# Message passing over a sorted graph on one core: table products in 36 of 40 steps, and one masking per five gathered tiles

## The reference

```python
h = relu(layernorm(x))
att = sigmoid(h[src] @ W_att[:d] + h[dst] @ W_att[d:] + b_att)
messages = (h[src] @ W_msg + b_msg) * att
aggregated = segment_sum(messages, dst, num_segments=num_nodes)
gi = aggregated @ W_ih.T + b_ih
gh = h @ W_hh.T + b_hh
r = sigmoid(i_r + h_r); z = sigmoid(i_z + h_z); n = tanh(i_n + r * h_n)
h_new = (1 - z) * n + z * h
out = x + gamma * (h_new - mean(h_new)) * rsqrt(var(h_new) + eps) + beta
```

## Time and profile before

| | |
|---|---|
| runs | 2367.26 us median of 3 (2366.56 to 2371.25) |
| the profiled execution | 2366.6 us |
| its span, first to last instruction | 2364.5 us |
| mean granted TensorE clock | 0.905 of full speed |
| busy share | PE 89%, DVE 83%, ACT 82%, POOL 75% |
| first gather of the 1600 starts, last one starts | 151.3 us, 2302.1 us |

### The profile page before, as it was taken

The page is one execution under the profiler, slowest core; times in us unless marked ns, Lnnn a source line. Parts: engine busy times, 40 slices in busy tenths (PEclk is TensorE's granted clock), DMA queues, the critical chain, the costliest instruction groups (busy, mean ns, idle before and its releaser), DMA issues.

```text
span 2364.5 us, 52153 instructions
## 1 busy us (share of the span) xinstructions
PE 2099.6 (89%) x17348; PEld 2019.7 (85%) x17348; DVE 1971.8 (83%) x4410; ACT 1931.7 (82%) x6704; POOL 1761.8 (75%) x1713
## 2 busy tenths in 40 slices
PE   3527999999999999999999999999999999999987
PEld 3426989989989989989989989989989989989977
DVE  6948888888888888888888888888888888888874
ACT  2378989989989989989989988989989989989934
POOL 5777777777777777777777777777777777777770
PEclk9856989989989989989989989989989989989988
DMA  9942222222222222222222222222222222222245
GB/s 172 276 99 72 58 63 61 59 62 61 61 63 64 59 62 61 59 62 61 59 62 62 63 62 61 59 62 61 59 62 62 61 64 62 58 63 60 58 124 202
DMA packets 175040, 178.53 MB, mean 76 GB/s; under 512 B 85953, under 2 KB 137203, under 8 KB 174643
## 3 DMA queue, kind: packets, MB, share of 16 engines
q0 software_dynamic: 54272, 112.04, 21.4%
q1 hardware_dynamic: 114121, 60.96, 10.0%
q10 hardware_dynamic: 6378, 2.18, 0.7%
HBM read 148.71 MB, written 26.33 MB: 74 GB/s over the span
## 4 chain that ended last, share of the span: by engine, by line
PE 59%; ACT 23%; DVE 8%; issue 4%; POOL 3%; DMA 2%; ACTq 1%; DVEq 0%; POOLq 0%
PE ps L1429 36%; ACT big L889 18%; PE ps L1414 9%; PE ps L1424 8%; ACT gate_ring L885 4%; POOL big L751 2%; PE ps L1435 2%; PE ps L1436 2%; DVE big L1181 2%; DMA row_ring<-node_table,set_idx 2%; DVE gate_ring L1165 1%; POOL row_ring L760 1%; PE ps L1438 1%; PE ps L1437 1%; DVE n_blk L1192 1%
## 5 line engine op out<-in xcount | busy, mean ns | idle before, releaser
L760 POOL DMA_INDIRECT row_ring<-node_table,set_idx x1600 | 1658.2, 1036 | 493.8 <-issue 380.3
L889 ACT ACTIVATE big<-set_score,big 128x128 f32<-128x128 f32 x4704 | 1506.6, 394 | 109.0 <-PE ps L1429 108.8
L1429 PE MATMUL ps<-big 128*128 128x128 f32 x9408 | 1366.8, 285 | 0.0
L1429 PEld LDWEIGHTS ps<-big 128*128 128x128 f32 x9408 | 1196.1, 197 | 0.0
L1181 DVE TENSOR_TENSOR big<-ps,big 128x784 f32<-128x784 f32 x768 | 743.2, 968 | 5.4 <-ACT big L889 2.8
L1414 PE MATMUL ps<-gate_ring,row_ring 128*128 128x64 f32 x3200 | 611.0, 275 | 119.7 <-DVE gate_ring L1165 118.9
L1165 DVE SCALAR_TENSOR_TENSOR gate_ring<-lane,set_rel,gate_ring 128x64 f32<-128x64 f32 x1600 | 453.2, 283 | 295.6 <-ACT gate_ring L885 287.9
L885 ACT ACTIVATE gate_ring<-set_win,row_ring 128x64 f32<-128x64 f32 x1600 | 537.0, 342 | 192.4 <-DMA row_ring<-node_table,set_idx 171.6
L1414 PEld LDWEIGHTS ps<-gate_ring,row_ring 128*128 128x128 f32 x3200 | 521.3, 205 | 178.7 <-DVE gate_ring L1165 171.5
L1424 PE MATMUL ps<-key_hot,lo_hot 128*128 128x196 bf16 x3072 | 411.0, 258 | 45.2 <-DVE big L1181 26.0
L1151 DVE TENSOR_TENSOR key_hot<-lane_key,set_key 128x1568 bf16<-128x1568 bf16 x384 | 372.2, 969 | 0.0
(11 more groups left out here) (124 smaller groups left out, 936.4 us busy)
## 6 DMA issues: line engine op xcount, KB each, us to landing
row_ring<-node_table,set_idx POOLq DMA_INDIRECT x1600
big<-in_x_dram SPq DMA_DIRECT2D x48, 256.0 KB, 6.1
h_blk<-hT_spill SPq DMA_DIRECT2D x97, 64.0 KB
node_table<-big SPq DMA_DIRECT2D x24, 258.0 KB
hT_spill<-big SPq DMA_DIRECT2D x24, 256.0 KB, 5.7
out_dram<-big SPq DMA_DIRECT2D x24, 256.0 KB
set_win<-dst_scores SPq DMA_DIRECT2D x160, 32.0 KB
set_score<-dst_scores SPq DMA_DIRECT2D x48, 64.0 KB, 2.9
```

The lines of the kernel that those rows point to most:

```text
L760: nc.gpsimd.indirect_dma_start(row_ring[:, t % ROWS_RING, :], None, table, bass.IndirectOffsetOnAxis(ap=set_idx[:, t // SET % 2, t % SET:t ...
L889: return nc.scalar.activation(a_buf[b % 2][:, h, :], set_score[:, b % 2, :], ACT.Sigmoid, bias=m_all[:, h, D:ROW])
L1429: return nc.tensor.matmul(ps[:, AM_BANK, 0:P], m_all[:, h, 0:D], a_buf[b % 2][:, h, :], start=h == 0, stop=h == HI - 1)
```

## The change

- **Products and gates in 36 steps.** `PARTS` goes from 32 to 36, `DENSE_AT` from 8 to 7. The table products are made in steps 3 to 38, two or three in each. ScalarE's gates for block u + 1 begin at step 7 of unit u and end at step 2 of unit u + 1.
- **`keep_block`** moves from step 38 of the same unit to step 1 of the next, ahead of the last `keep_pairs`.
- **One masking per five tiles.** `mask` (128x64 in f32, one per tile) is replaced by `make_masks` (is-equal over five tiles, 128x320, bf16 in and out, into `mask_ring`) and `gate_masks` (128x320, bf16 mask times f32 gates in place). `make_masks` of tiles 5m to 5m + 4 stands at the step of tile 5m + 2, `gate_masks` at that of tile 5m + 5, and TensorE's five `scatter` of them at that of tile 5m + 6. Before, tile t was masked and multiplied at its own step.
- **Rings.** `row_ring` has 13 buffers for 10, `gate_ring` 10 for 8. A group's sum is added one tile later (`GROUP_LAG`).
- **Destinations in bf16**, each twice, in the same bytes: four copies of 128x400 in the set-up (L800) become eight.

```diff
-PARTS = 32
+PARTS = 36
 PARTS_AT = 3
-DENSE_AT = 8
-GROUP_LAG = 3
+DENSE_AT = 7
+GROUP_LAG = 4
+MASKS = 5
...
-ROWS_RING = 10
-GATES_RING = 8
+ROWS_RING = 13
+GATES_RING = 10
...
+def masks_at(u, s, lag):
+
+    t = SPARSE - LAST_TILES + s if u == BLOCKS else tile_at(u, s)
+    return (t - lag) // MASKS - 1 if t is not None and t % MASKS == lag and MASKS <= t < SPARSE + MASKS else None
...
+def dense_at(u, s):
+
+    return (u + 1, s - DENSE_AT) if s >= DENSE_AT else (u, s + STEPS_U - DENSE_AT)
...
 def slices_of(part, total):
-    more = total % PARTS
-    first = part * (total // PARTS) + min(part, more)
-    return range(first, first + total // PARTS + (part < more))
+    return range(part * total // PARTS, (part + 1) * total // PARTS)
...
-                    if u + 1 < BLOCKS and s >= DENSE_AT:
-                        i = s - DENSE_AT
+                    b, i = dense_at(u, s)
+                    if 0 < b < BLOCKS and i < PARTS:
...
-            def mask(t):
-                dve.wait_ge(gates_ready, t + 1)
-                hot = gate_ring[:, t % GATES_RING, :]
-                nc.vector.scalar_tensor_tensor(out=hot, in0=lane[:, :], scalar=set_rel[:, t // SET % 2, t % SET:t % SET + 1],
-                                               in1=hot, op0=ALU.is_equal, op1=ALU.mult).then_inc(masks_ready, 1)
+            def make_masks(m):
+                first = 2 * (m * MASKS % SET)
+                rel = set_rel[:, m * MASKS // SET % 2, first:first + 2 * MASKS]
+                wait_reuse(dve, masks_ready, m - 1)
+                nc.vector.tensor_tensor(
+                    mask_ring[:, m % 2, :, :, :],
+                    lane_key[:, 0:WIN].rearrange("p (h w) -> p h w", w=2).unsqueeze(1).broadcast_to((P, MASKS, WIN // 2, 2)),
+                    rel.rearrange("p (j w) -> p j w", w=2).unsqueeze(2).broadcast_to((P, MASKS, WIN // 2, 2)),
+                    ALU.is_equal).then_inc(masks_made, 1)
+
+            def gate_masks(m):
+                dve.wait_ge(masks_made, m + 1)
+                dve.wait_ge(gates_ready, (m + 1) * MASKS)
+                at = m * MASKS % GATES_RING
+                hot = gate_ring[:, at:at + MASKS, :]
+                nc.vector.tensor_tensor(hot, mask_ring[:, m % 2, :, :, :].rearrange("p j h w -> p j (h w)"), hot, ALU.mult
+                                        ).then_inc(masks_ready, 1)
...
-                        mask(t)
+                        if t % MASKS == 2:
+                            make_masks(t // MASKS)
                         if t % GROUP == GROUP_LAG and t > GROUP:
                             add_group(t // GROUP - 1, bases[t // GROUP - 1])
+                    m = masks_at(u, s, 0)
+                    if m is not None:
+                        gate_masks(m)
...
+                    if s == 1 and u > 1:
+                        keep_block(u - 2)
...
-                    if s == STEPS_U - 2 and u:
-                        keep_block(u - 1)
...
-                pe.wait_ge(masks_ready, t + 1)
+                pe.wait_ge(masks_ready, t // MASKS + 1)
...
-                    t = tile_at(u, s)
-                    if t is not None:
-                        scatter(t)
+                    m = masks_at(u, s, 1)
+                    if m is not None:
+                        for t in range(m * MASKS, (m + 1) * MASKS):
+                            scatter(t)
```

More of the change, by code:

```diff
@@ L152, in gnn_program @@
     assert TILES % 2 == 1 and SPARSE < TILES and FINE <= P and GROWS <= P and HI <= P and 5 * GROWS <= 512 and KEYS <= 256
-    assert SPARSE % SET == 0 and GROUPS % 2 == 0 and DENSE_AT + PARTS == STEPS_U and SETS > 2 and TILES % 16 == 5
+    assert SPARSE % SET == 0 and SET % MASKS == 0 and GROUP % MASKS == 0 and GATES_RING % MASKS == 0 and LAST_TILES % MASKS == 0 and GROUPS % 2 == 0 and DENSE_AT + PARTS < STEPS_U + 4 and PARTS_AT + PARTS < STEPS_U and SETS > 2 and TILES % 16 == 5
     assert B_FIRST < HI and first_tile(1) >= GATES_EARLY and ZEROED <= D0 and -(-STEPS // 5) <= WIN and all(
@@ L161, in gnn_program @@
     idx_dram = nc.dram_tensor("sparse_src", (P, SPARSE), U32, kind="Internal").ap()
-    rel_dram = nc.dram_tensor("sparse_dst", (P, SPARSE), F32, kind="Internal").ap()
+    rel_dram = nc.dram_tensor("sparse_dst", (P, 2 * SPARSE), BF16, kind="Internal").ap()
     lo_dram = nc.dram_tensor("dense_lo", (P, QTILES), BF16, kind="Internal").ap()
@@ L288, in gnn_program @@
         set_idx = sb("set_idx", [P, 2, SET], U32)
-        set_rel = sb("set_rel", [P, 2, SET])
+        set_rel = sb("set_rel", [P, 2, 2 * SET], BF16)
         set_lo = sb("set_lo", [P, 2, PAIRS_B], BF16)
@@ L295, in gnn_program @@
         gate_ring = sb("gate_ring", [P, GATES_RING, WIN])
+        mask_ring = sb("mask_ring", [P, 2, MASKS, WIN // 2, 2], BF16)
         lo_hot = sb("lo_hot", [P, 2, BATCH // 2, P, 2], BF16)
@@ L381, in gnn_program @@
         gates_ready = sem("gates_ready")
+        masks_made = sem("masks_made")
         masks_ready = sem("masks_ready")
@@ L580, in _ @@
                     sp.dma_start(idx_dram, idx_cols.bitcast(U32)).then_inc(sparse_stored, 16)
-                    sp.dma_start(rel_dram, rel_cols).then_inc(sparse_stored, 16)
+                    sp.dma_start(rel_dram, rel_cols.bitcast(BF16)).then_inc(sparse_stored, 16)
                 if c == 21:
@@ L798, in keep_edges @@
                     c, j = e % 4 // 2, 5 * (e % 2)
-                    cols = (idx_cols.bitcast(U32) if e < 4 else rel_cols)[:, c * GROWS * GROUP:(c + 1) * GROWS * GROUP]
-                    nc.scalar.copy(cols.rearrange("e (p j) -> e j p", j=GROUP)[:, j:j + 5, :],
-                                   ps[:, bank, 0:5 * GROWS].rearrange("e (j p) -> e j p", p=GROWS)).then_inc(edges_kept, 1)
+                    turned = ps[:, bank, 0:5 * GROWS].rearrange("e (j p) -> e j p", p=GROWS)
+                    cols = slice(c * GROWS * GROUP, (c + 1) * GROWS * GROUP)
+                    if e < 4:
+                        nc.scalar.copy(idx_cols.bitcast(U32)[:, cols].rearrange("e (p j) -> e j p", j=GROUP)[:, j:j + 5, :], turned
+                                       ).then_inc(edges_kept, 1)
+                    else:
+                        twice = rel_cols[:, cols].bitcast(BF16).rearrange("e (p j w) -> e j p w", j=GROUP, w=2)
+                        for w in range(2):
+                            last = nc.scalar.copy(twice[:, j:j + 5, :, w], turned)
+                        last.then_inc(edges_kept, 1)
                 elif e < 10:
@@ L924, in _ @@
                         gate(t)
-                    if u + 1 < BLOCKS and s >= DENSE_AT:
-                        i = s - DENSE_AT
+                    b, i = dense_at(u, s)
+                    if 0 < b < BLOCKS and i < PARTS:
                         if i == 0:
-                            act.wait_ge(score_loaded[(u + 1) % 2], 16 * ((u + 1) // 2 + 1))
-                        if u:
-                            act.wait_ge(block_parts, (u - 1) * PARTS + (i + 1))
+                            act.wait_ge(score_loaded[b % 2], 16 * (b // 2 + 1))
+                        if b > 1:
+                            act.wait_ge(block_parts, (b - 2) * PARTS + (i + 1))
                         for h in slices_of(i, HI):
-                            last = dense_gate(u + 1, h)
+                            last = dense_gate(b, h)
                         if i == PARTS - 1:
@@ L1264, in _ @@
                     dve.wait_ge(agg_zeroed, 8)
+            keep_block(BLOCKS - 1)
             for k in range(len(JOB_AT), len(JOBS)):
```

2 lines of the change are left out of this document (1 added, 1 removed).

## The result

| | runs | median, us | lowest to highest |
|---|---|---|---|
| after | 20 | 2358.99 | 2353.70 to 2370.41 |
| before, same chip | 20 | 2369.44 | 2365.74 to 2374.53 |

The ratio is 0.996, 95% interval 0.9951 to 0.9968: faster by 0.4%, where I had forecast slower by 0.9%. The time lies in the range, 30 us under the predicted one, and on the side that I gave 26%. The profiled execution has a span of 2353.9 us, 10.6 less than before.

A forecast was written before the change was run, and what follows sets the result against it. GpSimd's back-to-back gathers were taken as the bound, 44.4 us a unit. Collisions at +0.54 us a unit gave +25 us, the start +1, the end -4: +22 us, 2389 us on the median, range 2345 to 2425.

The forecast's parts named there:

- What bounds the kernel: GpSimd's back-to-back gathers, 1.340 us each, set 44.4 us a unit; the other engines could do it in under 43.
- The clock "off the path": Each unit's 6.8 us stretch of TensorE at 1.2 GHz: neither losing nor gaining it moves the end.
- 36 steps at 0: Products and gates in 36 steps only even out the load of engines waiting for GpSimd: 0 on the path.
- How gathers are held: A gather starting during a VectorE operation with two SBUF inputs waits for its end, less 0.13 us; 3.1 us a unit.
- the two new prices: Cost to the gathers per unit: gate_masks (0.485 us long) +0.31 us, make_masks (0.317 us long) +0.09 us.
- One-hots close up, +0.24: Without a mask between, key_hots starts sooner after lo_hots and hits more gathers: +0.24 us a unit, bounds 0 and +0.38.
- The start: First waits of GpSimd for TensorE: more buffers save some, release in fives takes some back; +1 us, bounds -6 and +4.
- The end: More of the last block's products come before the last batch of tiles: -4 us, bounds 0 and -10.
- Rival 5: TensorE's chain was the bound after all, as the page says: 94 us less, 2273 us; chance 10%.
- Rival 2: Fewer collisions: VectorE's waits in fives give one-hots a good fixed phase to the gathers; 2342 us; chance 16%.
- Rival 4: GpSimd gets to wait for buffers, TensorE's waits in fives bringing more 1.2 GHz stretches; 2555 us with two more; chance 7%.
- Rivals 1 and 3: 1: gathers stay the bound and collide more, 2374 to 2412 us, 54%. 3: net nothing, 2369 us, 13%.

The follow-up runs named there:

- experiment 5: Every fifth gather left out: of the kernel before, 2367.53 us, ratio 0.9999; of the kernel before with only the 36 steps, 2155.04 us, ratio 0.9101.
- steps_only_2: Kernel before with only the 36 steps and the moved keep_block, old masks and rings: first run 2356.03 us, ratio 0.995; repeat 2355.59 us, ratio 0.9947.
- hots_first: Kernel before with lo_hots and key_hots of a step moved ahead of its mask: 2368.04 us, ratio 0.9999.
- thin_before_2: Kernel before with every fifth gather left out, its tile using rows of an earlier one: 2367.53 us, ratio 0.9999.
- experiment 6: Kernel before with extra f32 matmuls per tile in the light steps: two, 2359.93 us; one, 2359.00; two with every fifth gather left out, 2272.51.
- masks_only: Kernel before with masks in fives, five-tile scatters and larger rings, but the old 32 steps and keep_block place: 2369.45 us against 2367.71, ratio 1.0009.
- align_steps2_b: Kernel before with the 36 steps alone, VectorE waiting before lo_hots and key_hots for the gather two tiles ahead to land: 2323.04 us, ratio 0.9813.
- the group at 2761 us: Four runs on a chip where the kernel before took 2761.13 us: two with every fifth gather left out, 2442.24 and 2429.16; two with one-hots tied to gathers, 2780.71 and 2812.44.

## Why the prediction was wrong, by its steps

**What bounds the kernel: the step that failed.** I wrote that the three other engines "can do a unit in under 43 us and are held at 44.4 by the gathers". They could not. Two limits stood side by side. The loop of TensorE, ScalarE and VectorE took 44.37 us with its stretch at 1.2 GHz in each unit, and took it as well with a fifth of the gathers gone (experiment 5). The gathers, free of it, take about 44.1: 44.07 per 33.125 in `steps_only_2`, 44.11 after the change. The change shortened the loop to 39.0 us, as measured with a fifth of the gathers gone, and left the gathers as the bound, so that of 5.4 us a unit only some 0.3 were paid out. That is the -12.6 us.

Three readings led me wrong:

- *"GpSimd never waited for a buffer"*: the gap of 0.305 us was constant, but the duration of a gather is elastic. It holds waits for VectorE, whose operations keep time with the loop. In `hots_first` the durations fell by 0.009 us each, 14 us in all, and waits for buffers rose by 14, at the same pace. My sum, 33.125 x 1.340 = 44.4, proved nothing: it holds for any engine without idle time, whoever sets the pace. How GpSimd's phase came to rest where the hits filled out the loop's unit exactly is argued from this, not shown.
- *The 42.96 us of unit 1*. I took it for the free pace, ended when GpSimd's lead ran out. `thin_before_2` has no such shortage of gathers and goes 43.53, 44.18, 44.27, 44.31, 44.35 us. The first units are short by themselves, and one of them is no measure of a steady state.
- *ScalarE's 101.8 us of waits for products*. They were 43 waits of up to 4.2 us in 45 units, one a unit: the mark of a loop that waits for itself. I quoted the total and went on. After the change they are 20 us.

**The clock "off the path": wrong with it.** I had the stretch in the earlier trace rows and gave it no price because the gathers were to be the bound. With it gone (experiment 6) the loop is at least 2.1 us shorter, even with the extra matmuls in it, and the kernel 8 us faster. The Trainium skill (TensorE: Matmul & The Clock Gate, "HAM oscillation — how this bites in real kernels") describes a loop that is throttled anew in each round after its waits; the 45 stretches of before agree, though here the cause was steps without products, and giving TensorE something to do in them was the cure. My thought that waits in fives might bring more stretches is not refuted by the fall from 45 stretches (307 us) to 38 (188 us), for that is the 36 steps' doing: with the 36 steps alone there are 25 and 26 stretches, 99 and 109 us, in `steps_only` and `steps_only_2`, so the masks in fives did bring some back. What these cost, with the gathers as the bound, is not shown.

**36 steps at 0: wrong**, -12 us (`steps_only`, ratio 0.995).

**How gathers are held: right for the operations that mattered**, and so were the two new prices. `gate_masks` takes 491 ns (0.485 forecast), `make_masks` 317 (0.317). A hit, in the changed kernel, GpSimd's row (start, us, what) and then VectorE's:

```profile
662.01 1.25 POOL L772 DMA_INDIRECT row_ring<-node_table,set_idx  x1 [0.30 <-issue]
```

```profile
661.96 0.49 DVE L1196 TENSOR_TENSOR gate_ring<-mask_ring,gate_ring 128x320 f32<-128x320 bf16 x1 [1.07 <-ACT gate_ring L904]
```

The gather starts with 0.44 of the mask left and takes 0.31 more than 0.94. Over 46.55 units (1542 gathers) `gate_masks` cost 12.7 us, 0.27 a unit for +0.31; `make_masks` 0.7, 0.02 for +0.09; the masks removed gave back 2.6, 0.06 for 0.10.

**One-hots close up, +0.24: wrong in sign**, -0.53 a unit. It was built on the hits of before as a fixed cost. `masks_only` and `hots_first` lower them too, and gain nothing; they count only once the gathers are the bound. I had also written of random phase that "the measured 3.1 says that the formula holds". It matched in the sum alone, by accident: `lo_hots` cost 1.61 us a unit where the formula gives 0.92, `key_hots` 1.33 where it gives 2.10. After the change the gathers lose 2.7 us a unit in all, in `align_steps2_b` 2.1.

**The start**: +1.4 us for +1. **The end**: +0.4 for -4. The last gather in the chain lands 8.39 us after its start there, near the 8.21 of the earlier trace rows. Before, TensorE went on at 2302.42, right behind the mask of the landed tile, and the end was 62.1 us away. After, the chain passes from `gate_masks` over a job on VectorE to a reload of `h_blk`, and TensorE goes on 7.9 us behind the mask, with 53.3 us to the end. So 8.8 us of work had moved ahead, and the wait for the reload took it back. That is read from the two chains; no run tried it. The chain near the end, in the changed kernel:

```profile
2282.45 8.39 DMA row_ring<-node_table,set_idx
2290.92 0.23 ACT gate_ring L904
...
2292.18 0.49 DVE gate_ring L1196
...
2293.88 6.66 DMA h_blk<-hT_spill
2300.58 0.49 PE ps L1471 x2
```

**The rivals.** Rival 5, TensorE's chain as the bound after all (10%), had the kernel before right. But it priced the change from the 42.96 us of unit 1 and took 41.2 us a unit as the floor, by gathers that are never held, and so came to 2273. With the gathers' measured 44.1 as the floor it would have given about 2354. Rival 2 (16%) names what the trace after shows, fewer hits, but neither their source, for `steps_only` has them without waits in fives, nor why they pay: `hots_first` had the same mean gather in the old steps, and the time of before. Rival 4 did not come: from 225 us on the longest wait for a buffer after is 1.3 us. Rivals 1 and 3 fell with their common ground. The lower end of rival 1's own range does not follow from its terms either: with the one-hots at 0, the start at -6 and the end at -10 they give 2365, not 2374.

## What to carry to other kernels

An engine without gaps isn't thereby the bound: if its instructions contend with others, their durations stretch until it fits the pace that somebody else sets. Take a fifth of its work away and look whether the time moves; here one such run would have shown that it doesn't. Two limits within 1% of each other have to be moved both, or the second takes most of the gain: 4.7 us of loop bought 0.3 us a unit. Here the loop lost TensorE's clock once per round. Spreading TensorE's work into the light steps kept the clock in most rounds, and once the gathers were the bound, moving the VectorE operations that hold them gave another 33 us. Which limit stands first can differ from chip to chip, as the group at 2761 us shows.

## What the runs showed of the hardware

- Two idle-filling f32 matmuls behind each of some six tiles a unit, about 3 us of work by their start times, took the stretches at 1.2 GHz from 45 to 4, and the thinned loop from 44.37 to 42.26 us. One such matmul left 31 stretches and gained as much within the interval.
- The clock's fall and the loop were tied to each other: 45 stretches of 6.83 us, in before and in `thin_before_2` alike, units of 44.35 and 44.37 us with a deviation of 0.3 us. The stretches follow each other at 44.373 us, the same in both kernels and to within 0.001 us from one to the next. That looks as if the loop kept time with the clock; it is not tested. Freed of it, with the gathers as the bound, units vary by 1.2 to 2.3 us.
- A gather that starts during a VectorE operation with two SBUF inputs is held by what is left of it less 0.13 us, in f32 and in bf16, down to the 0.49 us of `gate_masks`. The Trainium skill's page (SBUF — State Buffer, "Who interferes with whom") names two SBUF inputs as the condition, and the 78 hits of `gate_masks` (12.7 us) agree.
- A gather that starts together with such an operation, or a little behind its start, is not held; the VectorE operation takes longer instead. After the change ten gathers started 0.004 to 0.042 us into a `gate_masks`: each took 0.94 to 0.95 us, and the masks took 0.53 to 0.57 us for 0.49. The eight that started 0.049 to 0.076 us into one took 1.22 to 1.26 us, and the masks 0.48 to 0.49. For `lo_hots` and `key_hots` after the change the border lies lower: the ten gathers that started up to 0.018 us into one were not held, and the operations took 0.04 to 0.06 us longer, while those from 0.031 us on were held. For the 128x64 masks of before it lies higher: none of the 132 gathers that started in their first 0.1 us was held, but 78 of the 100 that started 0.10 to 0.15 us into one were, by some 0.03 us. The gather at 1041.18 beside the mask at 1041.17 is of the first kind, so it did not show that masks hold no gather.
